# A 128-step recurrence on one core: VectorE's loop unrolled by four, a shorter tanh, and triangles and a bias on ScalarE

## The reference, cut to what matters

```python
def step(prev_h, xw_t):                       # the recurrence: 128 steps, one after the other
    next_h = jnp.tanh(xw_t + prev_h @ Wh)
    return (next_h, next_h)
...
xw = jnp.einsum('ntd,dh->nth', x, Wx) + b     # x: 8 x 128 x 128, Wx and Wh: 128 x 128
x = x + _L0_attn_ref(_L0_cond_ref(x, cond_1024, ...), ...)   # latent attention, 16 heads, 8 batches
x = x + _L0_ffn_ref(_L0_cond2_ref(x, ...), ...)              # a gated scan, then 6 layers of local attention and FFN
```

## Time and profile before

| what | us |
|---|---|
| median of three runs | 3383.85 (3377.65 to 3384.16) |
| the profiled execution, its own time | 3381.28 |
| its span, first to last instruction | 3379.5 |
| granted TensorE clock, mean | 0.984 of full speed |
| recurrence loop, first to last step's end | 55.4 to 2043.5 |

### The profile page before, as it was taken

One profiled execution on the slowest core, in us unless ns is written; L12 is line 12 of the kernel. 1 busy time (PEld: TensorE's weight loads), 2 busy tenths in 40 slices (PEclk: granted clock), 3 DMA queues, 4 the chain that ended last, 5 costly groups with the idle time before them and its releaser, 6 DMA issues.

```text
span 3379.5 us, 54177 instructions
## 1 busy us (share of the span) xinstructions
PE 2812.6 (83%) x12991; PEld 1717.5 (51%) x13101; DVE 2809.4 (83%) x8061; ACT 2171.9 (64%) x4492; POOL 2593.7 (77%) x2804
## 2 busy tenths in 40 slices
PE   5777778777787877878777788969999999999997
PEld 2333333333333333333333336746767777777676
DVE  5999999999999999999999994337777777777875
ACT  4666666666666666666666663336666666666665
POOL 8888888888888888888888881038778778778773
PEclk9999999999999999999999998879999999999999
DMA  1000000000000000000000002000010101000000
GB/s 33 0 0 0 0 0 0 0 0 0 0 0 0 0 0 0 0 0 0 0 0 0 0 0 73 1 1 1 0 36 0 36 0 36 0 32 4 0 0 7
DMA packets 21860, 21.97 MB, mean 7 GB/s; under 512 B 6334, under 2 KB 19396, under 8 KB 21060
## 3 DMA queue, kind: packets, MB, share of 16 engines
q1 hardware_dynamic: 21828, 21.55, 2.0%
HBM read 21.02 MB, written 0.52 MB: 6 GB/s over the span
## 4 chain that ended last, share of the span: by engine, by line
DVE 54%; PE 21%; issue 15%; ACT 4%; POOL 3%; DVEq 2%; SPq 0%; DMA 0%; POOLq 0%; ACTq 0%
DVE bank L1017 13%; PE bank L1322 5%; DVE bank L1012 3%; DVE bank L989 3%; DVE rot_s L1235 3%; DVE sq L989 3%; DVE rot_c L1235 3%; DVE ss L1238 3%; PE bank L1564 2%; DVE qT L998 2%; PE bank L1642 2%; DVE fix_trace L1083 2%; PE bank L1426 2%; PE bank L1616 2%; DVE sq L1075 2%
## 5 line engine op out<-in xcount | busy, mean ns | idle before, releaser
L1017 DVE TENSOR_REDUCE bank<-qkv_w 128x2 f32<-128x766 f32 (+1 forms) x768 | 912.7, 1219 | 120.6 <-issue 64.9
L739 ACT COPY qkv_w<-bank 128x512 f32<-128x512 f32 x258 | 218.2, 846 | 356.9 <-PE bank L1322 356.9
L667 POOL TENSOR_TENSOR qk<-rot_c,rot_s 128x512 f32<-128x512 f32 x192 | 256.8, 1337 | 207.8 <-DVE rot_s L1235 207.8
L1322 PE MATMUL bank<-diag_h,w_part 128*128 128x512 f32 x1024 | 307.2, 421 | 118.2 <-DVE bank L1012 106.9
L585 POOL TENSOR_TENSOR diag_h<-eye,part 128x512 fp32r<-128x512 f32 x384 | 393.9, 1040 | 0.0
L578 POOL TENSOR_TENSOR qkv_w<-b,offset 128x512 f32<-128x512 f32 x258 | 269.1, 1043 | 160.4 <-ACT b L721 150.0
L1327 PE MATMUL bank<-kT,wx 128*128 128x512 f32 x516 | 277.0, 618 | 136.3 <-ACT b L721 136.3
L1322 PE MATMUL bank<-diag_x,w_part 128*128 128x512 f32 x1032 | 385.6, 495 | 0.0
L1337 PE MATMUL bank<-qT,wh 128*128 128x256 f32 (+1 forms) x768 | 254.6, 467 | 95.6 <-DVE qT L998 95.6
L674 POOL TENSOR_TENSOR rs<-rs,halfs 128x8 f32<-128x8 f32 x192 | 320.1, 1667 | 16.0
L716 ACT ACTIVATE diag_x<-eye,X 128x128 fp32r<-128x128 f32 x1036 | 327.7, 389 | 1.4 <-DVE X L1110 1.4
(11 more groups left out here) (237 smaller groups left out, 6697.5 us busy)
## 6 DMA issues: line engine op xcount, KB each, us to landing
qkv_w<-in_L_ffn_Wqkv SPq DMA_DIRECT2D x6, 1536.0 KB
o_w<-in_L_ffn_Wo SPq DMA_DIRECT2D x6, 512.0 KB
w<-in_L_ffn_W SPq DMA_DIRECT2D x6, 341.0 KB
b<-in_L_ffn_b SPq DMA_DIRECT2D x6, 341.0 KB
w<-in_L_ffn_W SPq DMA_DIRECT2D x6, 128.0 KB
x_tok<-in_x SPq DMA_DIRECT2D x1, 512.0 KB
masks<-in_masks SPq DMA_DIRECT2D x1, 512.0 KB, 3.8
out<-o_fin SPq DMA_DIRECT2D x1, 512.0 KB, 3.2
```

The source lines that it names most:

```text
L667: pool.tensor_tensor(o, c_, s_[:, :, ::-1, :], ALU.add).then_inc(rot_sum, 1)
L1017: return dve.tensor_reduce((sum_h, sum_x)[n][:, a:b], chain[n][:, a:b, 0:LINKS], AX_X, ALU.add)
L1322: return pe.matmul(dst, w_part[:, n, w], diag[n][:, d, a:b, :].rearrange("p n k -> p (n k)"), start=start, stop=stop or n == 0, skip_group ...
```

## The change

It does six things, all in the recurrence.

1. VectorE's loop runs 32 times over four steps instead of 128 times over one. `rnn_op` is cleared once in four steps.
2. VectorE makes the triangles of batches 0 and 1 alone. Those of 2 and 3 come from ScalarE, first in its step (`triangle_mid`, two activations of 128x128, signal `tri_h_mid`), and TensorE waits for them between its two products of 256 columns.
3. The bias is added to x's sum on ScalarE (signal `x_biased`); `sum_x` now lies in SBUF.
4. ScalarE's first `take_sums_x` stands ahead of `place_rests_h(0)`, no longer behind it.
5. tanh has 26 operations instead of 33. The upper and lower parts of the denominator and of z are taken from the same wider arrays that the series' parts need (96 for 72 elements, 24 for 8), and the selection for small arguments is one predicated copy behind the last scan.
6. Several small arrays move between SBUF and PSUM (`f_guess`, `z_part` to SBUF, `c_upper`, `f_part` to PSUM), and constants for them are set by VectorE instead of GpSimd before the loop.

```diff
-                for m in range(2):
-                    rows = slice(2 * m, 2 * m + 2)
-                    dve.tensor_tensor(tri[0][:, rows, :], ... h_own[:, rows] ...).then_inc(tri_h_first, 1)
+                dve.tensor_tensor(tri[0][:, 0:2, :], ... h_own[:, 0:2] ...).then_inc(tri_h_first, 1)
...
+            def triangle_mid():
+                for n in (2, 3):
+                    ins = act.activation(tri[0][:, n, :], upto[:], ACT.Copy, scale=h_now[:, n:n + 1])
+                ins.then_inc(tri_h_mid, 1)
...
+                act.wait_ge(h_static, this)
+                triangle_mid()
                 place_guess_h(0, counts[0])
                 place_guess_h(1, counts[1])
                 act.wait_ge(split_h, this)
                 lower_h()
                 place_minus_h(counts[0])
-                place_rests_h(0, counts[0])
                 act.wait_ge(sum_placed[1], counts[1])
                 take_sums_x(0, counts[2])
+                place_rests_h(0, counts[0])
                 place_rests_h(1, counts[1])
+                act.wait_ge(x_scanned, this)
+                act.activation(xw[:], sum_x[:], ACT.Identity, bias=rnn_b[:], scale=1.0).then_inc(x_biased, 1)
                 take_sums_x(1, counts[3])
                 diagonals_x(around, 1)
-                act.wait_ge(x_scanned, this)
...
-                for m in range(2):
-                    pe.wait_ge(tri_h_first, counts[m])
-                    ins = sums_h(0, 2 * m, 2 * m + 2)
-                ins.then_inc(sum_ready[0], 1)
+                pe.wait_ge(tri_h_first, this)
+                sums_h(0, 0, 2)
+                pe.wait_ge(tri_h_mid, this)
+                sums_h(0, 2, 4).then_inc(sum_ready[0], 1)
...
-            with dve.Fori(0, T) as t:
+            with dve.Fori(0, T // UNROLL) as turn:
                 count[0] = 0
                 dve.sem_clear(rnn_op)
+                for u in range(UNROLL):
+                    t = UNROLL * turn + u
...
-                    step(dve.tensor_scalar(xw[:], sum_x, rnn_b[:], None, ALU.add))
+                    dve.wait_ge(x_biased, this)
...
-                n_u = upper(z_upper[:], z)
-                upper(z_part[:, :, 0], z)
-                n_s = step(dve.scalar_tensor_tensor(out=small_x, in0=big, scalar=0.0, in1=pre, ...))
+                n_u = upper(z_part[:, :, 0], z)
+                n_b = step(dve.tensor_scalar(small_z, f_keep[:, :, 0, 1], SMALL_SQ, None, ALU.is_lt))
...
-                n_d = upper(den_upper[:], den)
-                upper(den_part[:, :, 0], den)
-                n_e = tt(den_part[:, :, 1], den, den_upper[:], ALU.subtract)
-                n_b = tt(q0_big, q0, big, ALU.mult)
-                tt(q_keep[:, :, Q_TERMS - 1], rc, big, ALU.mult)
-                tt(q_seq[:, :, Q_TERMS - 1], q0_big, small_x, ALU.add)
...
-                dve.tensor_tensor_scan(q_trace ..., q_keep ..., q_seq ..., 0.0, ALU.mult, ALU.add).then_inc(h_made, 1)
+                n_q = step(dve.tensor_tensor_scan(q_trace ..., q_keep ..., q_seq ..., 0.0, ALU.mult, ALU.add))
+                after(n_q)
+                dve.copy_predicated(h_own, small_z.bitcast(I32), clamped).then_inc(h_made, 1)
```

More of the change, by code:

```diff
@@ L69 @@
 LINKS = 3 * D - 1
+UNROLL = 4
 def constants():
@@ L260, in program @@
         h_now = sb("h_now", [P, NB])
-        den_upper = sb("den_upper", [P, NB])
-        den_part = own(1, NB, 2)
+        den_part = f_part[:, 2:3 * NB:3, 3, :]
         quot_part = sb("quot_part", [P, NB, 2])
-        clamped, rc, q0, nq, small_x = (own(0, NB) for _ in range(5))
-        q_tmp = sb("q_tmp", [P, 4, NB])
+        clamped, nq = (own(0, NB) for _ in range(2))
+        rc = q_keep[:, :, Q_TERMS - 1]
+        q_tmp = sb("q_tmp", [P, 3, NB])
         diag = [tile[:] for tile in diag_tiles]
@@ L958, in _ @@
             dve.tensor_copy(h_own, condT[:]).then_inc(h_made, 1)
+            for block_, series in enumerate(BLOCKS):
+                for r in range(3):
+                    dve.memset(c_upper[:, :, block_, r:r + 1], parts_of(series[r + 1], -(1 << CLEAR[block_][r]))[0])
+            dve.memset(own_signs[:, 0:1], 1.0)
+            dve.memset(own_signs[:, 1:2], -1.0)
             dve.memset(f_keep, 0.0)
@@ L1028, in tanh @@
             def tanh():
-                xc, big, q0_big, xt = (q_tmp[:, n, :] for n in range(4))
+                xc, small_z, xt = (q_tmp[:, n, :] for n in range(3))
                 cells = [P, NB, 3, 3]
@@ L1045, in tanh @@
-                n_u = upper(z_upper[:], z)
-                upper(z_part[:, :, 0], z)
-                after(n_b)
-                n_s = step(dve.scalar_tensor_tensor(out=small_x, in0=big, scalar=0.0, in1=pre, op0=ALU.is_equal,
-                                                    op1=ALU.mult))
+                n_u = upper(z_part[:, :, 0], z)
+                n_b = step(dve.tensor_scalar(small_z, f_keep[:, :, 0, 1], SMALL_SQ, None, ALU.is_lt))
                 after(n_u)
-                n_v = tt(z_part[:, :, 1], z, z_upper[:], ALU.subtract)
+                n_v = tt(z_part[:, :, 1], z, z_part[:, :, 0], ALU.subtract)
@@ L1073, in tanh @@
+                after(n_l)
+                n_p = tt(rest_seq.rearrange("p (m k) (r c) -> p m (k r) c", k=3, c=3)[:, :, :, 1:3],
+                         f_part.rearrange("p m k c -> p m (k c)")[:, :, 0:6].unsqueeze(3).to_broadcast([P, 3 * NB, 6, 2]),
+                         z_part[:].unsqueeze(2).to_broadcast([P, 3 * NB, 6, 2]), ALU.mult)
                 after(n_p)
@@ L1111, in _ @@
             open_step(1)
-            with dve.Fori(0, T) as t:
+            with dve.Fori(0, T // UNROLL) as turn:
                 count[0] = 0
-                this, two = value(dve, t + 1), value(dve, 2 * t)
-                counts = [value(dve, two + n) for n in (1, 2, 3, 4)]
-                quarters = [value(dve, 4 * t + n) for n in (1, 2, 3, 4)]
-                def placed_h(m):
-                    dve.wait_ge(rest_placed[0], quarters[m])
-                    if m % 2 == 0:
-                        dve.wait_ge(minus_placed[m // 2], this)
-                dve.sem_clear(rnn_op)
-                placed_x(counts[0])
-                fold(1, 0, 4)
-                for half in range(2):
-                    difference_h(half, counts[half])
-                placed_x(counts[1])
-                fold(1, 4, 8).then_inc(x_scanned, 1)
-                placed_h(0)
-                fold(0, 0, 2)
-                placed_h(1)
-                fold(0, 2, 4)
-                dve.wait_ge(x_scanned, this)
-                step(dve.tensor_scalar(xw[:], sum_x, rnn_b[:], None, ALU.add))
-                placed_h(2)
-                fold(0, 4, 6)
-                placed_h(3)
-                after(step(fold(0, 6, 8)))
-                after(tt(pre, xw[:], sum_h, ALU.add))
-                tanh()
-                open_step(value(dve, t + 2))
@@ new lines, in _, with placed_h @@
+                dve.sem_clear(rnn_op)
+                for u in range(UNROLL):
+                    t = UNROLL * turn + u
+                    this, two = value(dve, t + 1), value(dve, 2 * t)
+                    counts = [value(dve, two + n) for n in (1, 2, 3, 4)]
+                    quarters = [value(dve, 4 * t + n) for n in (1, 2, 3, 4)]
+                    def placed_h(m):
+                        dve.wait_ge(rest_placed[0], quarters[m])
+                        if m % 2 == 0:
+                            dve.wait_ge(minus_placed[m // 2], this)
+                    placed_x(counts[0])
+                    fold(1, 0, 4)
+                    for half in range(2):
+                        difference_h(half, counts[half])
+                    placed_x(counts[1])
+                    fold(1, 4, 8).then_inc(x_scanned, 1)
+                    placed_h(0)
+                    fold(0, 0, 2)
+                    placed_h(1)
+                    fold(0, 2, 4)
+                    placed_h(2)
+                    fold(0, 4, 6)
+                    placed_h(3)
+                    after(step(fold(0, 6, 8)))
+                    dve.wait_ge(x_biased, this)
+                    after(tt(pre, xw[:], sum_h, ALU.add))
+                    tanh()
+                    open_step(value(dve, t + 2))
```

62 lines of the change are left out of this document (29 added, 33 removed).

## The result

| | us |
|---|---|
| the kernel before, same chip, median of four runs | 3384.01 (3377.65 to 3386.61) |
| the changed kernel, median of four runs | 3417.15 (3413.39 to 3420.37) |
| ratio, 95% interval | 1.0101 [1.0085, 1.0117] |
| its profiled execution: own time, span | 3413.39, 3411.6 |
| granted TensorE clock of that execution, mean | 0.942 of full speed (before 0.984) |

The change makes the kernel 33 us slower; the forecast was 3330, and the time lies outside the range, on the side that had a chance of 0.08.

What follows compares the result with a forecast made beforehand. VectorE was taken as the bound, with a nearly equal chain through TensorE and ScalarE beside it. The clamp at 10.28 plus 4.84 and 0.10 gave 15.22, mean step 15.24 against 15.66: 54 us off, 3330 us, range 3312 to 3362.

Steps and rivals of the forecast that it cites:

- Triangles on ScalarE: ScalarE's two triangles at the step's start: ready at 0.92 us, signalled at 0.99, wanted by TensorE at about 1.08.
- the term of the guesses: ScalarE's copies of the guesses stay where they were: first from 1.71 to about 2.67 us, second ending at 3.53.
- rests copied (L754): ScalarE's copy of h's first rests: wanted at 5.82 us, made from 5.89, 0.07 late by the reorder.
- h's first fold: VectorE's fold 0.61 us behind the rests' copy: at 6.50 against 6.91 before, its wait growing from 0.26 to 0.4.
- clamp to the next copy: The tanh stretch up to the next copy to `h_now`: 4.84 us before, plus 0.10.
- The new wait at the guesses: VectorE, ready at 2.44 us, gets the first guess at 2.74; of 0.84 saved, 0.48 arrive at the second difference.
- rival B: ScalarE's triangles or guesses come later; with 0.3 us more, the step is 15.45 and the time 3357; chance 0.15.
- Bias: Leaves VectorE between the folds, saving 0.13 us a step; costs nothing on ScalarE, done 3 us before it is read.
- tanh: Seven operations fewer change the step by +0.10 us: +0.20 for the predicated copy, -0.07 and -0.03 saved.
- C: tanh costs its upper end, up to +0.35 us more a step: 3375 us; chance 0.08.
- Rival D: In tanh the operation count matters: partly, 3290 us, chance 0.06; wholly, 3174 us, chance 0.02.
- Rival A: VectorE's 233-instruction loop no longer stays on chip, each return waits for a fetch: 3408 or 3485 us; chance 0.08.

Runs made afterwards that it cites:

- e1: The changed kernel plus five added 128-row TensorE products of 512 columns behind x's last product, results unread: 3325.71 us, ratio 0.9838.
- e3: The kernel before with only ScalarE's first copy of x's running sums moved ahead of h's first rests: 3441.59 us, ratio 1.0173.
- e11: The changed kernel plus five added TensorE products that use one row instead of 128: 3416.84 us, ratio 1.0083 to the kernel before.
- e2: The changed kernel with ScalarE's first copy of x's running sums put back behind h's first rests: 3345.36 us, ratio 0.9904 to the kernel before.
- e9: e1 with the old tanh of 33 operations and its buffers put back: 3311.1 us, ratio 0.9772 to the kernel before.
- e7: e1 with one step in VectorE's loop instead of four: 3340.2 us, ratio 0.9871 to the kernel before.
- e8: e1 with two added products instead of five: median 3327.86 us, ratio 0.9835 to the kernel before; one run took 3387.59.
- e12: The kernel before with only the unrolling and the bias on ScalarE, no added product: 3307.5 us, ratio 0.9785.

## Why the prediction was wrong

**The step that failed** is in "Triangles on ScalarE": "x's chain ends about 1.5 us earlier in a step that is 0.4 shorter: ScalarE is idle when h comes." The statement itself was right: ScalarE's wait before L724 is 0.85. But x's chain is TensorE's work too, and the prediction took its earlier end as harmless slack. Its own numbers give what this does to TensorE's wait: 0.76 + 1.5 - 0.4 = 1.86. Measured, x's last products end 13.72 behind the copy (1023.53 + 1.50 - 1011.31) where they ended 15.45 behind it (1024.60 + 1.49 - 1010.64), 1.73 earlier in a step that is 0.52 shorter at full clock, and the wait is 0.76 + 1.21 = 1.97. Behind it the products of h, which are on the path, ran wholly or in part at half the clock in 81 of 127 steps. What failed with it is the term of the guesses, "So they do not move": the second difference was forecast at 3.60 and follows at 4.50 in the slow step above. No rival had the clock, and the durations were all taken from a step at 1.00 as if that were fixed. The rows held what was needed to name the pause; that the clock would fall, and how often, could not be read from them.

The price: (15.86 - 15.18) x 127 = 86 us, the mean step of after less that of e1. The forecast of 3330 and these 86 make 3416, and 3417.15 was measured; e1, at full clock, measured 3325.71. The sum was thus right but for a term that it didn't have. That 3416 comes so close is in part luck: the step at full clock is 15.18 and not 15.24, worth 8 us, while the stages behind the recurrence, which the change does not touch, took 1341 us in this profiled execution and 1336 before. That the clock is the cause is shown from both sides: e1 gives it back and gains 91 us, e3 takes it away with one instruction moved, and e11, as e1 but with one-row products, gives back neither the clock nor the time.

Page and trace: The Trainium skill, page "TensorE: Matmul & The Clock Gate", section "What's actually happening", says that the lower clock is the default and that recent activity lifts it, between two levels; the 0.50 and 1.00 of these rows agree. Its section "HAM oscillation — how this bites in real kernels" describes a kernel whose clock falls again at the pause in every turn of its loop, a wait for DMA that is longer than the pauses here. In the changed kernel pauses of 1.94 to 2.14 us in a step of 15 to 17 were enough, though not in every step: 81 of 127.

**Term by term**, from the copy at 1011.31 in the step at full clock:

| term | forecast | measured |
|---|---|---|
| x's first fold | 0.77 | 0.78 |
| first and second difference | 2.74, 3.60 | 2.71, 3.56 |
| rests copied (L754) | 5.89 | 5.88 |
| h's first fold | 6.50 | 6.41 |
| clamp to the next copy | 4.94 | 4.96 |
| the step | 15.22 | 15.14 |

- *The new wait at the guesses*: there, 0.19 before L1025, released by L736, as named. The first fold, the differences and the rests came within 0.04. The wait before h's first fold is 0.28, forecast 0.4: the fold starts 0.53 behind L754 and not 0.61.
- *Triangles on ScalarE*: two take 0.69 and start 0.20 behind the copy. In time at full clock, so rival B did not come; e2 shows it as it would have been, without the reorder. The rests start at 5.88 without a wait behind L729, so the reorder holds them as forecast; that this costs 0.07 no run shows. Its real price was the clock.
- *Bias*: hidden on ScalarE, read long after it is made. The 0.13 shows in the time from h's first fold to the clamp: 10.18 - 6.41 = 3.77, forecast 3.78.
- *tanh*: forecast +0.10 a step; e1 against e9 gave 0.11 to 0.13, and 4.96 - 4.84 = +0.12 stands in the timelines. Rivals C and D are out.
- *Rival A, instruction fetch*: unrolling gives some 15 us (e7), and DMA from the second step to 2000 us reads:

```profile
DMA packets 1, 0.01 MB, mean 0 GB/s; under 512 B 0, under 2 KB 0, under 8 KB 0
```

One packet in some 30 returns, so there is no fetch at each of them with a body of 233 instructions, and rival A is out. Longer bodies were not tried.

Rival D was drawn from the Trainium skill, page "VectorE: DVE Perf Modes", section "Rules for kernel authors", which has one lower the count of operations and not that of semaphores. The runs disagree: 33 operations beat 26 by 14.6 us (e9). The eight removed gave back about 0.08 us a step (0.20 less 0.12, the wider arrays counted with them), and the one added, in a dependent pair of its own, took 0.20.

Open: why 81 of the 127 steps were slow and not all of them. The pause ahead of them does not tell: it is 1.94 to 2.14 in slow steps and 1.95 to 2.14 in the others. Open too: e8's one long run, and what a pause between the 1.69 us of e8's profiled execution, at full clock, and the 1.94 of the changed kernel does.

## What to carry to other kernels

When an edit brings work forward on the engine beside TensorE, ask what TensorE does afterwards: one pause grown from 0.76 to 1.97 us in a loop of 15 us cost 86 us here, while 2.87 us of idle time in four pieces cost nothing (e12). Read the granted clock by stretches of the loop, never from the page's tenths, and do not count products with one row as work that keeps it (e11). Operations of eight elements that stand in a dependent pair's gap were nearly free here: three of them took 0.09 us together. One behind the last scan is paid whole, 0.20.

## What the hardware showed that was not expected

- One pause that grows while the sum of idle time does not is enough: 3.11 us a step before, in pieces of 1.06 at most, and 3.11 in e3's step, with a piece of 2.00 and the clock at half behind it.
- A clock that falls inside a loop in which TensorE is busy for over 80% of the time: 1613.73 us of 1940 in the changed kernel at a clock of 0.93, against 1545.07 at 1.00 before.
- Five products with one row did not keep it up. e11's TensorE is busy for 1755.83 of 1940 us, more than e1's 1711.81, and has 0.93 where e1 has 1.00: 3416.84 against 3325.71 us.
- A predicated copy of eight elements takes 0.17 us on VectorE, and 0.20 from its start to that of the dependent copy behind it. Other operations of that size in such a pair, tanh's first two, start 0.20 apart too (1021.29 and 1021.49).
